# Feed-forward between two attentions: five f32 layers become three f16 products each

## The chip, the cores and the metric

One core of one Trainium2 chip runs the whole program in one launch. The metric is device time in microseconds (us). A core has five engines with a queue each: PE (TensorE: matmuls and transposes through it), DVE (VectorE), ACT (ScalarE), POOL (GpSimd) and SP (SyncE, here only issuing DMAs). They wait for each other through semaphores. A bank of PSUM holds 128 x 512 f32; PE writes there, DVE and ACT read there, POOL does not.

## The reference, cut to what matters

A sequence of 2048 tokens with 128 features goes through four blocks, each followed by a residual and a layer norm:

```python
x = layernorm(x + L0_attn(x))   # 16 heads of 64, causal
x = layernorm(x + L0_ffn(x))    # the part that is changed
x = layernorm(x + L1_attn(x))   # 16 heads of 8, with a Gaussian bias
x = layernorm(x + L1_ffn(x))
# L0_ffn, with tlin(x, w, s) = einsum('bsi,oi->bso', x, w) * s
h = silu(tlin(x, w1, s1)) * tlin(x, w2, s2)          # 128 -> 512, twice
h = gelu(tlin(h, h1, s_h1)); h = gelu(tlin(h, h2, s_h2))   # 512 -> 512, exact gelu
return tlin(h, w3, s3)                                # 512 -> 128
```

The weights are ternary times 8 in the inputs, but the kernel treats them as general f32.

## The kernel before

Three stages stand one after another, each a block of its own whose engines meet at its end.

**First attention.** Eight pairs of heads times four chunks of 512 queries are 32 units; a unit has 4, 8, 12 or 16 turns, one for each 128 keys, so that a pair has 40 turns and the stage 320. In a turn PE makes the scores (three f16 products for each of two heads, `ps_e`), one block of the row maxima of the next unit (`max_products`, bank pair `ps_x`, single: the next block waits until DVE has taken the last, `s_xf`), the product of an earlier turn's probabilities with v, and at most one operation in the bank `ps_y` (`use_y`). ACT makes the exponentials (`exps`, a ring of six buffers), POOL adds them up (`acc`, line L328), DVE reduces the blocks of maxima (`take_max`, L618 and L621) and masks diagonal scores (L697). `plan()` places the operations in `ps_y` by due turns: projections of the next pair (`qk`, `v`), the row sums (`sum`), the output products (`yo`), the turned maxima (`mt`, without which the next unit cannot start), and the transposes of the feed-forward weights (`wt`): eleven groups of four 128 x 128 transposes (w1 and w2 one group each, h1 and h2 four each, w3 one), due at turns 22 and 34 of the pairs 1 to 6. ACT copies a finished `wt` group from `ps_y` to SBUF in f32 and frees the bank; DVE has no part in it.

**Feed-forward.** Four chunks c of 512 tokens. `NH` is 4. For each chunk PE makes, in this order: four outputs of w1 and w2 (`gate_up`, 8 products of 128x128 by 128x512), four outputs of h1 from four inputs (`hidden(c, 0, o)`, 16 products), four of h2 (16), and w3 (`last_layer`, 4): 44 products of f32, 176 in the stage. Between them stand the norm before the next chunk (`n0`), the norm after the last one (`n1`), each with transposes to tokens and back, and the projections q, k, v, f of the second attention for the last chunk, which share one bank `ps_j`. ACT does silu, gelu and the copies of projections; DVE multiplies gate and up (`gated`, L1228), does the norms, `query`, `key`, `value` and the residual; POOL only splits the queries into three bf16 parts (L962 to L968). After the last chunk a chain of small steps prepares the second attention.

**Second attention and last feed-forward.** Not touched.

A line such as `link(ins)` adds one to a semaphore and makes DVE wait for it, so that the next DVE instruction starts only when this one has ended.

## Time and profile before

| | us |
|---|---|
| median of 3 runs | 1796.94 (1796.51 to 1797.92) |
| the profiled execution, its own time | 1798.3 |
| its span, first to last instruction | 1796.6 |
| first attention | 0 to 828 |
| feed-forward, PE's first product to its last | 835.4 to 1005.0 |
| preparation of the second attention | 1005 to 1046 |
| second attention and end | 1046 to 1796.6 |

The profiled execution is one run; 1.7 us of its time lie outside the span. A busy share is to be read by stage, since each stage has its own limit.

### The profile page before, as it was taken

What the parts mean: (1) busy time and instruction counts of PE and PEld (TensorE: products, weight loads), DVE (VectorE), ACT (ScalarE), POOL (GpSimd) and SP (SyncE); (2) the same over time, 40 slices, a digit from 0 to 9 for tenths busy, and PEclk for the clock granted to TensorE, in tenths of its full rate; (3) what the DMA queues carried; (4) which work ended last, traced back from release to release, by engine and by line L of the source; (5) the groups of instructions that cost most, each with busy time, mean ns of one, the idle gap of its engine ahead of it and who ended that gap; (6) DMA issues with size and microseconds to landing.
All of it is one profiled execution on the core that took longest, in us unless ns stands there. A gap on an engine that the chain in (4) does not pass through costs nothing.

```text
span 1796.6 us, 27707 instructions
## 1 busy us (share of the span) xinstructions
PE 1649.1 (92%) x10488; PEld 492.0 (27%) x10488; DVE 1277.0 (71%) x2570; ACT 965.8 (54%) x1109; POOL 670.0 (37%) x408
## 2 busy tenths in 40 slices
PE   7999999999999999995999769999999999999995
PEld 3232323333333323322444311111111111111122
DVE  6767576666667575722233489999999999999974
ACT  2444545444444444442343315777777777777774
POOL 4577877878887878892000110000000000000012
PEclk8999999999999999997999857999999999999998
DMA  4100000000000000001012440111211121111000
GB/s 112 35 9 13 14 13 9 12 13 10 16 7 19 8 16 10 13 13 31 2 36 58 100 94 1 24 24 24 41 24 31 31 46 26 24 23 24 2 2 24
DMA packets 76215, 46.40 MB, mean 26 GB/s; under 512 B 22158, under 2 KB 74930, under 8 KB 76082
## 3 DMA queue, kind: packets, MB, share of 16 engines
q1 hardware_dynamic: 74738, 43.38, 11.4%
q8 instruction: 83, 1.36, 0.3%
q10 hardware_dynamic: 1344, 1.25, 0.2%
q14 instruction: 50, 0.41, 0.1%
HBM read 25.66 MB, written 9.31 MB: 19 GB/s over the span
## 4 chain that ended last, share of the span: by engine, by line
PE 29%; DVE 17%; ACT 3%; DMA 2%; issue 1%; SPq 1%; POOL 0%; DVEq 0%; ACTq 0%; POOLq 0%
DVE maxpart L1717 15%; PE ps_o L1613 9%; PE ps_h L1013 6%; PE ps_r L1575 5%; ACT probs L1534 3%; PE ps_e L1603 2%; DMA qrows<-maxrow 2%; PE ps_g L995 1%; PE ps_u L1000 1%; PE ps_u L1022 1%; PE ps_r L1592 1%; SPq L1456 0%; PE ps_g L1091 0%; PE ps_r L1658 0%; PE ps_j L1044 0%
## 5 line engine op out<-in xcount | busy, mean ns | idle before, releaser
L1717 DVE TENSOR_REDUCE maxpart<-ps_r 128x1 f32<-128x512 f32 x1024 | 634.5, 682 | 26.8 <-PE ps_r L1575 25.9
L1534 ACT ACTIVATE probs<-ps_e 128x1024 f32<-128x1024 f32 x512 | 504.7, 1023 | 194.9 <-PE ps_e L1603 189.8
L328 POOL TENSOR_TENSOR acc<-acc,probs 128x1024 f32<-128x1024 f32 (+3 forms) x256 | 502.9, 1964 | 77.9 <-ACT probs L362 55.3
L362 ACT ACTIVATE probs<-ps_e 128x1024 f32<-128x1024 f32 (+1 forms) x320 | 285.7, 901 | 380.7 <-DVE ps_e L697 131.0
L1575 PE MATMUL ps_r<-krows,qrows 60*128 60x512 bf16 x1024 | 346.9, 402 | 50.8 <-DVE maxpart L1717 17.9
L528 PE MATMUL ps_o<-probs,v 128*64 128x512 f32 (+3 forms) x1280 | 308.6, 561 | 0.2 <-ACT pv_raw L369 0.2
L618 DVE TENSOR_REDUCE maxpart<-ps_x 128x2 f32<-128x1024 f32 x192 | 234.5, 1222 | 75.3 <-PE ps_x L443 75.3
L1603 PE MATMUL ps_e<-qrows,krows 62*128 62x512 bf16 x1024 | 278.8, 386 | 4.2 <-DMA qrows<-maxrow 3.3
L1613 PE MATMUL ps_o<-probs,v 128*9 128x512 f32 x2048 | 269.2, 598 | 12.4 <-ACT probs L1534 12.3
L1499 POOL TENSOR_TENSOR rstd<-veps,power 128x4 f32<-128x4 f32 x8 | 8.1, 1014 | 700.2 <-DVE veps L1767 700.2
L1575 PEld LDWEIGHTS ps_r<-krows,qrows 60*128 60x128 bf16 x1024 | 80.0, 94 | 466.2 <-DVE maxpart L1717 340.4
L621 DVE CUSTOM_DVE_ANT_0 masked<-ps_x,later 128x128 f32<-128x128 f32 (+3 forms) x256 | 115.0, 486 | 60.7 <-PE ps_x L443 59.6
L443 PE MATMUL ps_x<-k_hi,q_hi 64*128 64x512 f16 (+3 forms) x640 | 114.0, 353 | 20.0 <-DVE maxpart L618 16.1
L493 PE MATMUL ps_e<-q_hi,k_hi 64*128 64x512 f16 (+3 forms) x640 | 115.7, 358 | 0.4 <-ACT probs L362 0.3
L493 PE MATMUL ps_e<-q_hi,k_lo 64*128 64x512 f16 (+3 forms) x640 | 112.6, 348 | 0.0
L493 PE MATMUL ps_e<-q_lo,k_hi 64*128 64x512 f16 (+3 forms) x640 | 112.5, 348 | 0.0
L323 POOL TENSOR_TENSOR acc<-probs 128x1024 f32<-128x1024 f32 x32 | 75.3, 2353 | 98.8 <-ACT probs L362 98.8
L528 PEld LDWEIGHTS ps_o<-probs,v 128*64 128x64 f32 x1280 | 63.8, 135 | 86.9 <-issue 77.2
L493 PEld LDWEIGHTS ps_e<-q_hi,k_hi 64*128 64x128 f16 x640 | 30.8, 93 | 158.8 <-issue 103.9
L697 DVE TENSOR_TENSOR ps_e<-ps_e,ahead 128x256 f32<-128x256 f32 (+1 forms) x128 | 55.6, 443 | 23.7 <-PE ps_e L493 15.9
L1603 PEld LDWEIGHTS ps_e<-qrows,krows 62*128 62x128 bf16 x1024 | 59.3, 94 | 32.9 <-ACT probs L1534 10.9
L962 POOL CAST parts_q<-qs 128x512 bf16<-128x512 f32 x4 | 2.4, 609 | 176.1 <-DVE qs L1242 176.1
(258 smaller groups left out, 1368.6 us busy)
## 6 DMA issues: line engine op xcount, KB each, us to landing
qrows<-q_rows SPq DMA_DIRECT2D x64, 192.0 KB
rbc<-rden SPq DMA_DIRECT2D x128, 64.0 KB, 2.1
q_rows<-parts_q SPq DMA_DIRECT2D x24, 128.0 KB, 2.4
k_rows<-parts_k SPq DMA_DIRECT2D x24, 128.0 KB, 2.4
krows<-k_rows SPq DMA_DIRECT2D x16, 192.0 KB, 5.9
w_rows<-parts_w SPq DMA_DIRECT2D x6, 256.0 KB, 2.6
qrows<-a_rows SPq DMA_DIRECT2D x64, 24.0 KB
qrows<-w_rows SPq DMA_DIRECT2D x64, 24.0 KB
```

The lines of the kernel that those rows point to most:

```text
L328: pool.tensor_tensor(acc[:, u % 2, :, o:], acc[:, u % 2, :, o:], probs[:, turn % RING, :, o:], ALU.add)\
L362: act.activation(probs[:, turn % RING, :, o:], ps_e[:, turn % 2, :, o:], ACT.Exp, scale=1.0 / math.sqrt(D0))\
L443: mm = pe.matmul(ps_x[:, h, 0:w], hi["q"][rows, p % 2, (4 * qc + t) * P:(4 * qc + t + 1) * P], hi["k"][rows, p % 2, c * QC:c * QC + w], st ...
L493: mm = pe.matmul(out[:, h, o:], k_part["k"][rows, p % 2, keys], q_part["q"][rows, p % 2, queries], start=n == 0 and turn % 2 == 0, stop=n ...
L528: mm = pe.matmul(ps_o[D0 * h:D0 * h + D0, o:], v[:, p % 2, kt, D0 * h:D0 * h + D0], probs[:, turn % RING, h, o:], start=kt == 0, stop=kt = ...
L618: dve.reduce_max(maxpart[:, u % 2, :, t, c:c + 1], ps_x[:, :, 0:w], AX.X).then_inc(s_xf, 1)
L621: ins = dve.tensor_tensor_reduce(out=masked[:, h, 0:w], in0=ps_x[:, h, 0:w], in1=later[:, QC - w:QC], scale=1.0, scalar=-3e38, op0=ALU.add ...
L1534: act.activation(probs[:, HG * (turn % 2) + hh], ps_e[:, e % 2], ACT.Exp).then_inc(s_ex, 1)
L1575: return pe.matmul(out, qrows[64 * j:64 * j + R_M, u % 3, c, hh, t * P:(t + 1) * P], krows[64 * j:64 * j + R_M, u // NQ % 2, hh, c * KB:(c ...
L1603: mm = pe.matmul(ps_e[:, e % 2, j], krows[64 * j:64 * j + R_END, u // NQ % 2, hh, at * P:(at + 1) * P], qrows[64 * j:64 * j + R_END, u % 3 ...
L1613: mm = pe.matmul(ps_o[32 * hh:32 * hh + D1 + 1, :], v1[:, TU * j + at, HG * (u // NQ) + hh, :], probs[:, HG * (turn % 2) + hh, j, :], star ...
L1717: dve.reduce_max(maxpart[:, at:at + 1], ps_r[:, k, :], AX.X).then_inc(s_bf[k], 1)
```

## The change

All five layers of the feed-forward take three f16 products in place of one f32 product: high weights by high activations, low weights by high activations, high weights by low activations. A high part is the value rounded to f16, the low part what is left, rounded to f16.

Weights: after the transposes ACT writes the high part, and DVE, from the same bank, the low part; only then is `ps_y` free. DVE then also sums the squares of each weight row (`row_norms`), and at turn 296 PE adds these over the partitions (a new operation `bound`) and DVE works out, in a chain of fifteen linked instructions, scale factors that keep the hidden activations inside the range of f16 and folds them into the scales `sc`.

Activations: the input x is copied twice by ACT (f16, then f32) and its low part made by POOL. DVE writes gate times up to `prod` in f32 and then copies it to f16; POOL makes the low part. ACT writes each gelu in f32 and then again, scaled, in f16; POOL scales the f32 one and makes the low part. Rings of two buffers tie these together. PE makes outputs 0 and 1 of a hidden layer together, first all products with high activations, then those with low ones. `last_layer(c-1)` and the residual move behind the first output of the next chunk. The projections q and k now follow each other directly. POOL's splitting of queries comes after the low parts of each chunk.

```diff
@@ first attention: placing, ACT, PE, DVE
+            due.setdefault(TP * (NPAIR - 1) + 16, []).append(("bound", 0))
...
                 elif kind == "wt":
-                    out = wt[name][:, 0, :] if o is None else wt[name][:, :, o * P:(o + 1) * P]
+                    w_hi, w_full = weight_group(i, 0)
                     act.wait_ge(s_yp, n + 1)
-                    act.activation(out, ps_y[:, :] ..., ACT.Copy).then_inc(s_yf, 1)
+                    act.activation(w_hi, w_full, ACT.Copy).then_inc(s_fh, 1)
...
+                elif kind == "bound":
+                    pe.wait_ge(s_nr, 4)
+                    for t in range(4):
+                        for h in range(2):
+                            last = pe.matmul(ps_y[32 * t:32 * t + 32, 0:6 * NH], ones2[:, h, :], norms[...], ...)
...
+            def row_norms(name, o):
+                if name == "w3":
+                    # four tensor_tensor of 128x16 or less, in SBUF
+                    return
+                for t in range(NH) if o is None else (o,):
+                    row = raw[name][:, t, :]
+                    ins = dve.tensor_tensor_reduce(out=squares..., in0=row, in1=row, scale=1.0, scalar=0.0,
+                                                   op0=ALU.mult, op1=ALU.add, accum_out=norms[:, layer, t:t + 1])
+                ins.then_inc(s_sq, 1)
+            def bounds():
+                def inverse_root(out, src, w):
+                    link(dve.tensor_scalar(half[:, 0:w], src.bitcast(I32), 1, None, ALU.arith_shift_right))
+                    link(dve.tensor_scalar(out.bitcast(I32), half[:, 0:w], -1.0, float(ROOT_SEED), ALU.mult, ALU.add))
+                inverse_root(seed[:, 0:2], total[:, 4:6], 2)
+                link(dve.tensor_tensor(total[:, 4:6], total[:, 4:6], seed[:, 0:2], ALU.mult))
+                link(dve.tensor_scalar(most[:, 0:1], total[:, 0:1], float(DM * DM), None, ALU.mult))
+                link(dve.tensor_tensor(most[:, 3:4], most[:, 0:1], total[:, 2:3], ALU.mult))
+                link(dve.tensor_tensor(most[:, 1:2], most[:, 0:1], total[:, 4:5], ALU.mult))
+                link(dve.tensor_tensor(most[:, 2:3], most[:, 3:4], total[:, 5:6], ALU.mult))
+                inverse_root(seed[:, :], most[:, 0:3], 3)
+                link(dve.tensor_scalar(up[:, :], seed[:, :], 2.0 ** 15, None, ALU.mult))
+                link(dve.reciprocal(down[:, :], up[:, :]))
+                for n, col in (("w2", up[:, 0:1]), ("h1", down[:, 0:1]), ("h2", down[:, 1:2]), ("w3", down[:, 2:3])):
+                    link(dve.tensor_scalar(sc[n], sc[n], col, None, ALU.mult))
...
+                elif kind == "wt":
+                    dve.wait_ge(s_fh, i + 1)
+                    dve.tensor_tensor(w_lo, w_full, weight_group(i, 0)[0], ALU.subtract).then_inc(s_yf, 1)
+                    row_norms(*FGROUPS[i])
+                elif kind == "bound":
+                    dve.wait_ge(s_yp, n + 1)
+                    dve.reduce_sum(total[:, :], ps_y[...], AX.X).then_inc(s_yf, 1)
+                    bounds()
@@ feed-forward: POOL
+            def features_low(c):   # waits s_tf, s_xh
+                pool.tensor_tensor(x_part[:, 1, :], xt[:, CHUNK[c]], x_part[:, 0, :], ALU.subtract).then_inc(s_xl, 1)
+            def gated_low(c, o):   # waits s_ah
+                pool.tensor_tensor(a_part[:, 1, o, :], prod[:, n % 2, :], a_part[:, 0, o, :], ALU.subtract).then_inc(s_al, 1)
+            def hidden_low(c, k, o):   # waits s_ha, s_hl, then s_hu, s_hh
+                pool.tensor_scalar(gel_up[:, :], gel[:, n % 2, :], up[:, k + 1:k + 2], None, ALU.mult).then_inc(s_hu, 1)
+                pool.tensor_tensor(part[:, 1, o, :], gel_up[:, :], part[:, 0, o, :], ALU.subtract).then_inc(s_hl, 1)
@@ feed-forward: PE
+            def first_layer(out, name, c, o):
+                pe.matmul(out[:, :], w_hi, x_part[:, 0, :], start=True, stop=False)
+                pe.matmul(out[:, :], w_lo, x_part[:, 0, :], start=False, stop=False)
+                if o == 0:
+                    pe.wait_ge(s_xl, c + 1)
+                return pe.matmul(out[:, :], w_hi, x_part[:, 1, :], start=False, stop=True)
...
+            def hidden(c, k, outs):
+                for o in outs:
+                    if n >= 2:
+                        pe.wait_ge(s_ha, n - 1)
+                    for i in range(NH):       # o == 0: waits s_ah (k = 0) or s_hh (k = 1) for input i
+                        for part in range(2):
+                            pe.matmul(ps_h[n % 2][:, :], w[:, part, i, ...], src[:, 0, i, :], ...)
+                for o in outs:
+                    for i in range(NH):       # o == 0: waits s_al or s_hl
+                        mm = pe.matmul(ps_h[n % 2][:, :], w[:, 0, i, ...], src[:, 1, i, :], ...)
+                    mm.then_inc(s_h, 1)
...
             for c in range(NQ):
-                for o in range(NH):
+                gate_up(c, 0)
+                if c > 0:
+                    last_layer(c - 1)
+                for o in range(1, NH):
                     gate_up(c, o)
...
-                hidden(c, 1, 0)
+                hidden(c, 1, (0, 1))
                 if c > 0:
                     project("q", c - 1)
-                hidden(c, 1, 1)
-                if c > 0:
                     project("k", c - 1)
-                hidden(c, 1, 2)
+                hidden(c, 1, (2,))
@@ feed-forward: ACT and DVE
+                if n >= 2:
+                    act.wait_ge(s_hu, n - 1)
+                act.activation(gel[:, n % 2, :], ps_h[n % 2][:, :], ACT.Gelu, scale=...).then_inc(s_ha, 1)
+                act.wait_ge(s_ha, n + 1)
+                act.activation((b_part, c_part)[k][:, 0, o, :], gel[:, n % 2, :], ACT.Identity, scale=up[...]).then_inc(s_hh, 1)
...
+                if n >= 2:
+                    dve.wait_ge(s_al, n - 1)
+                dve.scalar_tensor_tensor(prod[:, n % 2, :], ps_u[m % 2][:, :], sc["w2"][...], gate[:, n % 2, :], ...).then_inc(s_gu, 1)
+                dve.wait_ge(s_gu, m + 1)
+                dve.tensor_copy(a_part[:, 0, o, :], prod[:, n % 2, :]).then_inc(s_ah, 1)
```

## Rows read from the trace of the kernel before

**Rows 1.** The page: busy time and share of each engine.

```profile
PE 1649.1 (92%) x10488; PEld 492.0 (27%) x10488; DVE 1277.0 (71%) x2570; ACT 965.8 (54%) x1109; POOL 670.0 (37%) x408
```

**Rows 2.** Busy time by stretch, first attention: from:to, length, engines, PE clock.

```profile
230.00:330.00 100.00, 97.98 (x726) 32.51 (x722) 64.75 (x141) 47.78 (x60) 79.85 (x42) 1.00 0.05 12
...
795.00:805.00 10.00, 6.91 (x40) 1.70 (x40) 0.69 (x1) 3.26 (x4) 9.71 (x5) 1.00 0.01 2
```

**Rows 3.** The same view, one chunk of the feed-forward.

```profile
884.40:927.40 43.00, 43.00 (x120) 20.32 (x119) 15.50 (x52) 18.02 (x25) 3.53 (x4) 1.00 0.14 37
```

**Rows 4.** The chain that ended last, in the feed-forward: start, length.

```profile
927.40 10.30 PE ps_h L1013 x24
```

**Rows 5.** Order of time, PE, f16 products in the first attention.

```profile
174.18 0.61 PE L422 MATMUL ps_y<-x_sb,wq_hi 128*128 128x512 f16 x2 [0.56 <-DVE k_lo L652]
174.63 0.38 PE L422 MATMUL ps_y<-x_sb,wq_lo 128*128 128x512 f16 x1
174.94 0.39 PE L493 MATMUL ps_e<-q_hi,k_hi 64*128 64x512 f16 x2
```

**Rows 6.** Groups by line and form, feed-forward: busy, mean ns, idle before.

```profile
L1228 DVE SCALAR_TENSOR_TENSOR act_a<-ps_u,sc_w,gate 128x512 f32<-128x512 f32 x16 | 12.0, 751 | 16.8 <-PE ps_u L1000 16.8
L1122 ACT ACTIVATE x_sb<-ps_h,sc_h 128x512 f32<-128x512 f32 x16 | 11.0, 687 | 35.6 <-PE ps_h L1013 35.6
...
L968 POOL TENSOR_TENSOR parts_q<-qs,parts_q 128x512 bf16<-128x512 f32 x3 | 3.5, 1155 | 0.2
...
L1249 DVE CAST parts_k<-mk 128x512 bf16<-128x512 f32 x3 | 2.5, 830 | 9.8 <-ACT mk L1134 9.8
...
L1213 DVE TENSOR_TENSOR t<-t,veps 128x4 f32<-128x4 f32 x8 | 1.3, 162 | 0.3
L1251 DVE CAST parts_k<-rest 128x512 bf16<-128x512 f32 x3 | 1.3, 426 | 0.1
```

**Rows 7.** The weight transposes by tile: count, duration, first and last start.

```profile
L464 PE MATMUL ps_y<-ident,raw_h x32: 272/273/329, 301.7 to 620.2; 128*128 128x128 f32 x32
...
L464 PE MATMUL ps_y<-ident,raw_w x12: 272/273/329, 204.6 to 690.3; 128*128 128x128 f32 x12
```

**Rows 8.** Order of time at a weight group of turn 22.

```profile
302.38 0.60 ACT L392 ACTIVATE wt_h<-ps_y 128x512 f32<-128x512 f32 x1 [0.69 <-PE ps_y L464]
...
303.36 1.23 DVE L618 TENSOR_REDUCE maxpart<-ps_x 128x2 f32<-128x1024 f32 x1 [0.65 <-PE ps_x L443]
...
305.02 0.22 PE L443 MATMUL ps_x<-k_hi,q_hi 64*128 64x128 f16 x2
...
306.33 2.35 POOL L323 TENSOR_TENSOR acc<-probs 128x1024 f32<-128x1024 f32 x1 [3.83 <-ACT probs L362]
```

**Rows 9.** Order of time at a weight group of turn 34.

```profile
325.30 12.35 POOL L328 TENSOR_TENSOR acc<-acc,probs 128x1024 f32<-128x1024 f32 x5
...
329.38 0.60 ACT L392 ACTIVATE wt_h<-ps_y 128x512 f32<-128x512 f32 x1 [0.57 <-PE ps_y L464]
...
330.35 1.23 DVE L618 TENSOR_REDUCE maxpart<-ps_x 128x2 f32<-128x1024 f32 x1 [2.38 <-PE ps_x L443]
...
331.91 0.38 PE L443 MATMUL ps_x<-k_hi,q_hi 64*128 64x512 f16 x2
```

**Rows 10.** Order of time: a DVE instruction in SBUF beside one of POOL.

```profile
35.96 2.34 POOL L323 TENSOR_TENSOR acc<-probs 128x1024 f32<-128x1024 f32 x1 [10.51 <-ACT probs L362]
35.99 3.40 DVE L687 TENSOR_SCALAR yt<-xt,obias 128x2048 f32<-128x2048 f32 x1
```

**Rows 11.** Groups by form, first attention: DVE with one operand in PSUM.

```profile
L621 DVE CUSTOM_DVE_ANT_0 masked<-ps_x,later 128x512 f32<-128x512 f32 x64 | 41.5, 685 | 22.6 <-PE ps_x L443 22.6
```

**Rows 12.** Order of time around turns 296 to 298.

```profile
759.49 12.36 POOL L328 TENSOR_TENSOR acc<-acc,probs 128x1024 f32<-128x1024 f32 x5
...
762.63 1.23 DVE L618 TENSOR_REDUCE maxpart<-ps_x 128x2 f32<-128x1024 f32 x1
...
766.49 0.38 PE L443 MATMUL ps_x<-k_hi,q_hi 64*128 64x512 f16 x2
```

More of the change, by code:

```diff
@@ L90, in build @@
         masked = sb("masked", [P, 2, QC])
+        squares = sb("squares", [P, NH, P], BF16)
+        norms = sb("norms", [P, 6, NH])
+        total = sb("total", [P, 6])
+        half = sb("half", [P, 3], I32)
+        seed = sb("seed", [P, 3])
+        most = sb("most", [P, 4])
+        down = sb("down", [P, 3])
         ahead = sb("ahead", [P, 2 * P])
@@ L465, in use_y @@
                                             else raw[name][:, o, t * P:(t + 1) * P], ident[:, :])
+                elif kind == "bound":
+                    pe.wait_ge(s_nr, 4)
+                    for t in range(4):
+                        for h in range(2):
+                            last = pe.matmul(ps_y[32 * t:32 * t + 32, 0:6 * NH], ones2[:, h, :],
+                                             norms[:, :, :].rearrange("p r o -> p (r o)"), start=h == 0, stop=h == 1,
+                                             skip_group_check=True)
                 elif kind == "sum":
@@ L876, in build @@
         J_FREE.update({("k", NQ - 1): J_AT["q", NQ - 1] + 1, ("v", NQ - 1): J_AT["q", NQ - 1] + 2})
-        U_W = {(c, o): 5 * c + o for c in range(NQ) for o in range(NH + 1)}
+        U_USES = []
+        for c in range(NQ):
+            U_USES += [(c, 0)] + [(c - 1, NH)] * (c > 0) + [(c, o) for o in range(1, NH)]
+        U_USES += [(NQ - 1, NH)]
+        U_W = {use: m for m, use in enumerate(U_USES)}
         CHUNK = [slice(c * QC, (c + 1) * QC) for c in range(NQ)]
@@ L969, in _ @@
                     .then_inc(s_pq, 1)
+            features_low(0)
+            for c in range(NQ):
+                for o in range(NH):
+                    gated_low(c, o)
+                for o in range(NH):
+                    hidden_low(c, 0, o)
+                for o in range(NH - 1):
+                    hidden_low(c, 1, o)
+                if c + 1 < NQ:
+                    features_low(c + 1)
+                hidden_low(c, 1, NH - 1)
+                if c > 0:
+                    query_parts(c - 1)
+            query_parts(NQ - 1)
         @block.tensor
@@ L987, in to_features @@
                 tr.then_inc(s_tp, 1)
+            def first_layer(out, name, c, o):
+                w_hi, w_lo = [wt_part[name][:, part, 0, o * P:(o + 1) * P] for part in range(2)]
+                pe.matmul(out[:, :], w_hi, x_part[:, 0, :], start=True, stop=False)
[3 more added lines that the diff above has]
+                return pe.matmul(out[:, :], w_hi, x_part[:, 1, :], start=False, stop=True)
             def gate_up(c, o):
@@ L1017, in last_layer @@
             def last_layer(c):
                 m = U_W[c, NH]
+                out = ps_u[m % 2]
                 pe.wait_ge(s_gu, m - 1)
                 for i in range(NH):
-                    pe.wait_ge(s_ha, 2 * NH * c + NH + i + 1)
-                    mm = pe.matmul(ps_u[m % 2][:, :], wt["w3"][:, i, :], act_c[:, i, :], start=i == 0, stop=i == NH - 1)
+                    pe.wait_ge(s_hh, 2 * NH * c + NH + i + 1)
+                    for part in range(2):
+                        pe.matmul(out[:, :], wt_part["w3"][:, part, i, :], c_part[:, 0, i, :], start=i == 0 and part == 0, stop=False)
@@ L1023, in last_layer @@
+                for i in range(NH):
+                    pe.wait_ge(s_hl, 2 * NH * c + NH + i + 1)
+                    mm = pe.matmul(out[:, :], wt_part["w3"][:, 0, i, :], c_part[:, 1, i, :], start=False, stop=i == NH - 1)
                 mm.then_inc(s_u, 1)
@@ L1071, in _ @@
                     project("v", c - 1)
-                hidden(c, 1, 3)
+                hidden(c, 1, (3,))
                 if c > 0:
                     project("f", c - 1)
-                last_layer(c)
+            last_layer(NQ - 1)
             c = NQ - 1
@@ L1279, in _ @@
             for c in range(NQ):
-                for o in range(NH):
+                gated(c, 0)
+                if c > 0:
+                    residual(c - 1)
+                for o in range(1, NH):
                     gated(c, o)
```

145 lines of the change are left out of this document (103 added, 42 removed).

## The prediction, made before the changed kernel was run

> **What bounds the kernel now.** I read the page first: PE is busy for 92% of the span, DVE 71%, POOL 37% [rows 1]. That is a mean over stages, so busy time by stretch comes next. In the middle of the first attention PE is busy 97.98 of 100 us, and POOL already 79.85 [rows 2]. Near its end PE falls to 6.91 of 10 while POOL is at 9.71: there POOL's sums set the pace [rows 2]. In the feed-forward a chunk takes 43.00 us and PE is busy for all 43.00; DVE has 15.50, ACT 18.02 and POOL only 3.53 [rows 3]. So a shorter product shortens this stage at once, until another engine's answer is late. The chain that ended last runs through these products with nothing between them [rows 4].
>
> **Products of the feed-forward.** A hidden output is 4 products, each two records. 24 records take 10.30 us [rows 4], 0.429 each, so one f32 product takes 0.858. An f16 product of the same shape starts 0.225 after the one before (three from 174.18 to 174.63), although one lasts 0.38 [rows 5]. If it took a quarter of the f32 product it would be 0.2146. These are the ends; I take 0.218, between them, because a steady stream should lose less than a group of three. The gain of a product is 0.858 - 3 x 0.218 = 0.204, times 176 = **-36.0 us**, with bounds -32.3 (0.225) and -37.8 (0.2146).
>
> The Trainium skill, "TensorE: Matmul & The Clock Gate", section "Back-to-back issue gap", gives 518 cycles at the full clock, 0.216 us, for 512 columns; the rows lie on both sides of it. By it the gain would be 37 us and the whole sum 1 us lower.
>
> **New waits there.** A result is out 0.16 after PE is free (0.38 - 0.22, [rows 5]) and its reader starts about 0.2 after. ACT needs 0.69 for a gelu and, I take, 0.69 again for the f16 copy; DVE 0.75 for gate times up and 0.43 for a copy, or 0.83 where POOL is running; POOL 1.155 for a difference [rows 6]. POOL's scaling is not in the trace: at least a DVE copy's 0.43, at most its own two-input 1.155; I take 0.6, nearer a one-input instruction. Then:
> - In chunk 0 PE's third product waits for POOL's first low part: two copies of 0.6 (as L392, [rows 8]) in a row and 1.155 put it some 1.2 late.
> - At the start of h1 the last f16 input is ready 0.2 + 0.75 + 0.05 + 0.85 = 1.85 after PE is free. Six products cover 1.3, transposes 0.4 from chunk 1 on. With DVE's 1.5 an output against PE's 1.3, that leaves 0.55 in chunk 0 and 0.6 in each later one.
> - Projection k now follows q in the same bank, with ACT's 0.69 between: 0.2 + 0.69 + 0.04 = 0.93, in three chunks. Before, a hidden output lay there.
> - Output 2 of a hidden layer waits for the gelu of output 0, covered but for 0.1, twice in a chunk.
> - POOL's query splitting delays the next chunk's low parts, 0.4 twice.
>
> At the start of h2 I count nothing: gelu and copy are ready 1.63 after PE is free, and six products with transposes cover 1.7; the low parts are needed after 4.5 and ready after 2.9. `last_layer` is hidden behind the next chunk's first output. Sum: 2.0 + 3 x 1.9 + 0.8 = **+8.5 us**, bounds 3 (only q to k) and 14 (POOL's scaling at 1.155). The preparation at 1005 to 1046 stays: its chain gets no new instruction, and POOL's two splits fit ahead of it.
>
> **Weight groups in the first attention.** Eleven groups, from 204.6 to 690.3 [rows 7], each now have 0.69 of DVE for the low part, then the squares: one instruction of 512 columns (0.68, as L621 of this width, [rows 11]), or four of 128 for w1 and w2. They stand ahead of DVE's next block of maxima, and the next block of PE waits for that one. Two positions repeat.
> - *Turn 22.* ACT's copy ends at 302.98. DVE then works to 303.7 and to 304.45, so the reduction that began at 303.36 begins at 304.5 and ends at 305.7; PE wanted the bank at 305.02 [rows 8]. Stall 0.85. POOL is idle until 306.33. Four h groups: 3.4; w1 1.05 (four short instructions take 0.9); w3 0.9. Together 5.35.
> - *Turn 34.* ACT's copy ends at 329.98, DVE's low part at 330.7, and without any other wait the stall would again be 0.85. But POOL is adding without a break, 2.47 per instruction: one runs from 330.24 to 332.6 [rows 9].
>
> Does the sum of squares wait for it? A DVE instruction that began 0.03 after one of POOL lasted 3.40 [rows 10]: POOL's end at 38.30, and 1.09 more, which is 2048 columns at the rate of L1251's 512 in 0.43 [rows 6]. So it stood until POOL had finished. The same copy takes 0.83 beside POOL and 0.43 alone [rows 6]. Both take two elements at once from SBUF. Instructions with one operand in PSUM are not touched: L621 is 0.685 at 80% POOL [rows 2, 11]. The squares read two streams from SBUF; no row shows such an instruction beside POOL. Bounds: no wait, or a wait for the end of POOL's instruction. I take the wait, since two SBUF elements per step is what the two delayed forms share. Then DVE gets to the squares at 332.6, the reduction ends at 334.4 instead of 331.57, and PE, which wanted the bank at 331.91 [rows 9], stalls 2.55. Four h groups: 10.2. In w2 the first of four short instructions waits likewise, POOL then takes one more addition of 2.35, after which it has no input, since PE has stopped: 5.2. Together 15.4, against 4.45 without the wait.
>
> The Trainium skill, "SBUF — State Buffer", section "SBUF: two separate sides", says that DVE and GpSimd share one pair of ports as an exclusive lock, held for a whole instruction, and that a DVE instruction with two SBUF inputs needs it too. The trace agrees for the two delayed forms (3.40 and 0.83) and has no row for two inputs. With the rule this part is 20.8 us, without it 9.8.
>
> **The chain of scales.** At turn 296 DVE is free at 763.86 [rows 12]; its reduction of PE's sums ends about 764.4. Fifteen linked instructions at 0.2 (0.16 and 0.04 idle, L1213, [rows 6]) are 3.0. Four are two-input ones in SBUF, and POOL is adding from 759.49 to 771.85 [rows 12]. Two of them wait, to 766.8 and 769.3; then POOL is out of input, because PE, wanting the bank at 766.49 [rows 12], waits for the reduction behind the chain. It ends at 771.5, the reduction at 772.75. PE loses 6.1, POOL, which sets the pace from here, **5.3**. Without the wait: 1.3.
>
> **Sum.** -36.0 + 8.5 + 20.8 + 5.3 = -1.4. The profiled execution took 1798.3, so 1796.9; it lies 1.4 above the median 1796.94. Carried to the median: **1795.5 us**.
>
> **Rivals.**
> - *DVE's two-input instructions don't wait for POOL* (0.20). For it: no row shows the wait in this form. Against it: rows 10 and the copies. Attention costs 9.8 + 1.3 = 11.1: -36.0 + 8.5 + 11.1 = -16.4, 1780.5 us.
> - *POOL becomes the bound of the feed-forward* (0.12), slower. Scaling at 1.155 makes 8 x 2.4 + 5 x 1.2 + 3.5 = 28.7 us of POOL in a chunk, and if some ten DVE instructions of 0.43 to 0.69 hold it up, 34 to 35, against PE's 43.00 - 44 x 0.204 = 34.0. From 34 on POOL decides, and late low parts stop PE at each layer; 3 us more a chunk, 12 in all: +10.6, 1807.5 us. Against it: the copies alone delay POOL by under 3 us.
> - *The clock falls* (0.05). It is 1.00 through the stage [rows 3]; waits of 1 to 2 us at each layer could lower it. If a quarter of its 142 us, 35, pass at half the clock, half of that is lost, 18: 1813.5 us. The 6 us wait at turn 298 is the likeliest place.
>
> **How the numbers follow.** The forecast has 0.63. Its own range is 1786 to 1803: products -1.8 to +3.7, waits +-5, attention +-5, put together +-8. The rivals carry it to **1778 to 1806**, which leaves out under 0.07 below and 0.13 above. A measurement tells from no change about 0.2%, 3.6 us. Of the forecast 0.23 lie more than that below, 0.28 within, 0.12 above; the first rival adds 0.19 below and 0.01 within, the second 0.01 within and 0.11 above, the third 0.05 above: faster 0.42, same 0.30, slower 0.28.
>
> **What would show it.** Feed-forward from PE's first product to its last: 142 us (169.6 before, less 36.0, plus 8.5), records of about 0.22, PE busy some 95%. k's product 0.9 after q's copy. The squares of h groups at turn 34 about 2.4 us long, at turn 22 0.6; PE idle before L443's counterpart 2.5 and 0.85. The scale chain 7 us long with two instructions of over 2 us. First attention 26 us longer; from the feed-forward's end to the end of the program no difference. I am wrong if the squares take 0.6 everywhere (then 1780), if PE doesn't wait on `ps_x` after them, or if low parts from POOL end PE's waits in the hidden layers.

## The result, and the profile after

The changed kernel takes 1810.68 us (median of 4, 1809.69 to 1811.82); the kernel before took 1797.26 in the same comparison. The ratio is 1.0075, 95% interval 1.0058 to 1.0092: slower by 13.4 us, and outside the predicted range of 1778 to 1806 with its 1795.5. The profiled execution took 1810.6, its span 1808.9. By stage, from the starts of the same instructions in both traces:

| stage | before | after | difference | predicted |
|---|---|---|---|---|
| first attention and norm, to the first product of the feed-forward | 835.4 | 866.0 | +30.6 | +26.1 |
| feed-forward, first to last product | 169.6 | 155.9 | -13.7 | -27.5 |
| preparation, to the first product of the slides | 16.6 | 15.9 | -0.7 | 0 |
| second attention and end | 775.0 | 771.1 | -3.9 | 0 |

The page of the changed kernel. Against [rows 1] POOL has gone from 37% to 43%. In `PEclk`, the granted clock of PE by slice, there are digits of 8 in slices 18 to 20, where the kernel before has 9, 7 and 9. A new group stands among the costliest, POOL's scaling.

```profile
PE 1626.2 (90%) x10680; PEld 476.3 (26%) x10680; DVE 1324.5 (73%) x2649; ACT 989.8 (55%) x1145; POOL 782.4 (43%) x492
...
PEclk8999999999999999988899856999999999999998
...
L1073 POOL TENSOR_SCALAR gel_up<-gel,up 128x512 f32<-128x512 f32 x32 | 51.3, 1603 | 21.2 <-ACT gel L1288 18.0
```

**First attention, turn 34.** Timeline of the changed kernel where it stands at an h group (start, us), to be read against [rows 9]:

```profile
333.08 7.60 POOL L351 TENSOR_TENSOR acc<-acc,probs 128x1024 f32<-128x1024 f32 x3
...
335.30 0.69 DVE L731 TENSOR_TENSOR wt_h_parts<-ps_y,wt_h_parts 128x512 f16<-128x512 f32 x1 [2.04 <-ACT wt_h_parts L414]
...
335.91 2.58 DVE L681 CUSTOM_DVE_ANT_0 squares<-raw_h 128x512 bf16<-128x512 f32 x1
...
338.42 1.22 DVE L646 TENSOR_REDUCE maxpart<-ps_x 128x2 f32<-128x1024 f32 x1
339.69 0.39 PE L464 MATMUL ps_x<-k_hi,q_hi 64*128 64x512 f16 x2 [2.32 <-DVE maxpart L646]
...
340.33 1.57 PE L556 MATMUL ps_o<-probs,v 128*64 128x512 f32 x4
```

The squares take 2.58 us where POOL is adding without a break, and 0.68 at turn 22 [rows 8], where it is idle; the reduction behind them is late and PE stands for 2.32. That is the forecast (2.4, 0.6, stall 2.5) within 0.2 us. The last line was not forecast: the four products with v take 1.57 us, not 1.08. Granted clock by stretch (the third number from the end; 1.00 is 2.4 GHz):

```profile
336.00:342.00 6.00, 3.68 (x22) 0.74 (x20) 5.20 (x5) 0.69 (x2) 4.54 (x2) 0.90 0.00 0
342.00:348.00 6.00, 6.00 (x42) 1.77 (x40) 3.71 (x9) 2.48 (x4) 4.44 (x3) 0.82 0.00 0
795.00:805.00 10.00, 9.76 (x45) 2.25 (x47) 4.19 (x12) 3.07 (x3) 6.27 (x4) 0.67 0.00 0
...
238.00:244.00 6.00, 5.94 (x36) 1.69 (x38) 2.92 (x9) 1.83 (x2) 2.62 (x2) 0.72 0.00 0
...
544.00:550.00 6.00, 6.00 (x50) 1.79 (x46) 4.98 (x11) 2.60 (x4) 3.71 (x2) 1.00 0.00 0
```

Behind four of the five stalls of turn 34 the mean clock of 6 us is 0.72: 3.4 us at the half level, 1.2 GHz, which cost 1.7 us each; the third h group (544 to 550) kept 2.4 GHz, after the same stall of 2.32. Behind the stall of the scale chain it is 0.67 over 10 us, which cost 3.3. So 10 us of the 30.6 are clock. The rest: PE's waits for DVE on `ps_x` between 200 us and the end of the stage rose from 6.3 to 29.2 us, by 22.9, and its waits for POOL at the end fell from 15.6 to 13.6. 22.9 + 10.1 - 2.0 = 31.0, against 30.6.

This sum takes only the places named. Over the whole stage, from its start and in steps of 1 us (PE's busy time, times what the granted clock lacks to 1.00), the clock cost 20.2 us, against 12.4 before: 7.7 more, because the opening, before 80 us, lost only 6.5 where it had lost 9.8. PE's waits on `ps_x` from the start rose by 24.3. 24.3 + 7.7 - 2.0 = 30.0. What the opening loses differs from trace to trace (8.0 in that of e1 below) without an edit there, so 2 to 3 us of such a difference can be chance.

**The scale chain.** Two instructions waited for POOL, the rest took 0.15 to 0.25; PE's stall is 6.38 us (6.1 forecast from [rows 12]):

```profile
786.45 2.37 DVE L696 TENSOR_SCALAR half<-total 128x2 int32<-128x2 int32 x1
...
789.05 2.23 DVE L700 TENSOR_TENSOR total<-total,seed 128x2 f32<-128x2 f32 x1
...
795.24 0.61 PE L464 MATMUL ps_x<-k_hi,q_hi 64*128 64x512 f16 x2 [6.38 <-DVE maxpart L646]
```

The first has one input, two int32 per partition.

**Feed-forward.** The stage as a whole, PE's waits in it (us in total, times, longest), and the timeline around the start of the second chunk:

```profile
866.00:1021.90 155.90, 138.68 (x618) 62.23 (x618) 67.20 (x181) 89.53 (x123) 118.96 (x93) 0.97 0.14 33
```

```profile
PE ps_h L1167 <- POOL x_sb L1076: 6.4, 4, 1.9
PE ps_g L1130 <- POOL x_part L1060: 4.8, 2, 4.0
PE ps_h L1157 <- DVE a_part L1401: 2.8, 5, 0.9
PE ps_j L1203 <- ACT mq L1298: 2.3, 3, 0.8
```

```profile
900.30 1.56 POOL L1073 TENSOR_SCALAR gel_up<-gel,up 128x512 f32<-128x512 f32 x1 [0.17 <-POOL c_part L1076]
...
901.95 1.15 POOL L1076 TENSOR_TENSOR c_part<-gel_up,c_part 128x512 f16<-128x512 f32 x1
903.06 1.15 POOL L1060 TENSOR_TENSOR x_part<-xt,x_part 128x512 f16<-128x512 f32 x1
...
904.27 0.61 PE L1130 MATMUL ps_g<-x_part,wt_w_parts 128*128 128x512 f16 x1 [4.02 <-POOL x_part L1060]
```

Before, PE was busy for all 169.6 us and POOL for 10.58 (the chunk in [rows 3] is typical); now PE is busy for 138.68 of 155.9 and POOL for 118.96. The products became as short as forecast (0.2156 apart, sixteen in 3.45 us, against half of the 0.429 between records in [rows 4]), but PE stands for 17.2 us, two thirds of it (11.6) for POOL. One hidden output costs POOL 1.56 + 1.155 and two waits, 2.97 us, against PE's 2.6. The scaling, taken as 0.6 and bounded by 1.155, took 1.56. The low parts of h2's inputs are late by 1.5 to 1.9 in each chunk. The low part of x for the second chunk is late by 4.02, and behind that the clock is at the half level until 907.3.

### The profile page after: what moved, and what is told of

The parts are those of the page before. It is cut to its first block, busy times and chain, and to the rows that moved or that the text cites. A ratio compares the mean times of both kernels' runs of the same rounds, so it can differ in the third digit from the quotient of the medians.

```text
span 1808.9 us, 28389 instructions
## 1 busy us (share of the span) xinstructions
PE 1626.2 (90%) x10680; PEld 476.3 (26%) x10680; DVE 1324.5 (73%) x2649; ACT 989.8 (55%) x1145; POOL 782.4 (43%) x492
## 4 chain that ended last, share of the span: by engine, by line
PE 22%; DVE 19%; POOL 4%; ACT 4%; issue 2%; DMA 0%; SPq 0%; DVEq 0%; POOLq 0%; ACTq 0%
DVE maxpart L1892 17%; PE ps_o L1788 9%; PE ps_r L1750 6%; ACT probs L1709 3%; POOL gel_up L1073 2%; PE ps_e L1778 2%; POOL x_sb L1076 1%; PE ps_h L1157 1%; PE ps_h L1167 1%; PE ps_r L1767 1%; POOL c_part L1076 1%; PE ps_g L1251 0%; PE ps_j L1203 0%; ACT gel L1288 0%; PE ps_r L1833 0%
## 5 line engine op out<-in xcount | busy, mean ns | idle before, releaser
L556 PE MATMUL ps_o<-probs,v 128*64 128x512 f32 (+3 forms) x1280 | 313.1, 569 | 0.2 <-ACT pv_raw L392 0.2
L1788 PE MATMUL ps_o<-probs,v 128*9 128x512 f32 x2048 | 268.4, 596 | 12.4 <-ACT probs L1709 12.2
L1073 POOL TENSOR_SCALAR gel_up<-gel,up 128x512 f32<-128x512 f32 x32 | 51.3, 1603 | 21.2 <-ACT gel L1288 18.0
```

The source lines that it names most:

```text
L556: mm = pe.matmul(ps_o[D0 * h:D0 * h + D0, o:], v[:, p % 2, kt, D0 * h:D0 * h + D0], probs[:, turn % RING, h, o:], start=kt == 0, stop=kt = ...
L1788: mm = pe.matmul(ps_o[32 * hh:32 * hh + D1 + 1, :], v1[:, TU * j + at, HG * (u // NQ) + hh, :], probs[:, HG * (turn % 2) + hh, j, :], star ...
```

## The experiments

Sixteen kernels ran; where nothing else is said, each is the changed kernel with one edit. Times are medians; ratios are to the kernel before, which took 1796.4 to 1797.6 beside them.

| run | us | ratio (95%) | edit |
|---|---|---|---|
| e1 | 1793.28 | 0.9977 (0.9967 to 0.9986) | one-input instruction for the squares |
| e2 | 1789.05 | 0.9953 (0.9938 to 0.9968) | squares by ACT |
| e3 | 1806.35 | 1.0053 (1.0038 to 1.0068) | scale chain in the feed-forward |
| e4 | 1797.85 | 1.0004 (0.9994 to 1.0013) | low parts of gelus by DVE |
| e5 | 1810.33 | 1.0075 (1.0059 to 1.0092) | POOL scales by a constant |
| e6 | 1800.49 | 1.0022 (1.0012 to 1.0031) | POOL scales by a two-input product |
| e7 | 1814.81 | 1.0101 (1.0086 to 1.0116) | k later, low part of x earlier |
| e12 | 1814.33 | 1.0096 (1.0082 to 1.0110) | k later |
| e8 | 1771.92 | 0.9862 (0.9847 to 0.9876) | e2, e3, e4 and k later |
| e9 | 1769.10 | 0.9844 (0.9831 to 0.9858) | e2, e3, e4 |
| e10 | 1767.98 | 0.9837 (0.9823 to 0.9850) | e9 with q earlier |
| e11 | 1766.11 | 0.9828 (0.9815 to 0.9842) | e10 with the chain split |
| e13 | 1813.35 | 1.0084 (1.0067 to 1.0101) | 32 bytes of SBUF unused |
| e14 | 1796.61 | 0.9992 (0.9982 to 1.0001) | kernel before, 32 bytes unused |
| e15 | 1763.43 | 0.9811 (0.9796 to 0.9825) | e11 with 32 bytes unused |
| e16 | 1763.44 | 0.9808 (0.9794 to 0.9823) | e11 with 96 bytes unused |

### Does DVE wait for POOL, and what does the clock add?

```diff
-                    ins = dve.tensor_tensor_reduce(out=squares..., in0=row, in1=row, ..., accum_out=norms[:, layer, t:t + 1])
+                    ins = dve.reduce_max(aside[:, layer, t:t + 1], row, AX.X)   # norms: constants
```

> In place of the sums of squares of weight rows stands, on the same engine at the same place, a maximum over the same 512 (or 128) elements: one SBUF input instead of two, about the same 0.68 us alone. The norms are then constants (the sum of squares is left out), everything else stays. Theory (DVE's two-input instruction waits until POOL's running instruction ends, and PE's stall at turn 34 of 2.32 us, 4.69 for w2, is followed by some 6 us of lower clock that cost 1.6 more): the instruction takes 0.6 to 0.7 us at turn 34 too, PE's stall there falls to about 0.3, the clock in the 6 us behind it is 1.00, and the kernel gains 4 x (2.0 + 1.6) + 5.5 = about 20 us: 1790. Rival (DVE simply has too much to do at that place): the stall stays near 2.3 and the time near 1810. Second rival (the lock is right but the clock would have fallen anyway): about 12 us gained, 1798.

Measured: 17.4 us less, between the 20 of the theory and the 12 of the second rival. The instruction, the sum of PE's waits on `ps_x`, and the stretches that had 0.90 and 0.82:

```profile
L683 DVE TENSOR_REDUCE aside<-raw_h x8: 674/676/677, 303.9 to 625.7; 128x1 f32<-128x512 f32 x8
...
PE ps_x L466 <- DVE maxpart L648: 17.0, 21, 6.4
...
336.00:342.00 6.00, 6.00 (x52) 1.89 (x50) 4.91 (x13) 1.88 (x4) 5.34 (x3) 1.00 0.00 0
342.00:348.00 6.00, 4.77 (x39) 1.57 (x37) 4.64 (x8) 3.38 (x5) 3.18 (x3) 1.00 0.01 3
```

Same place, same engine, same 512 elements, same load on POOL: all eight take 0.68, the stall behind one of them is 0.41, and the clock stays at 2.4 GHz. DVE's load is not the cause. Two things differ between the instructions: the squares have a second SBUF input, and they write 512 values to SBUF where the maximum writes one. Writing is not it: the low part at 335.30 above writes 512 values to SBUF while POOL is adding, and takes 0.69. Nor is it the form: the masked maxima of [rows 11] are of the same form as the squares, with one operand in PSUM, and take 0.685 beside POOL. That leaves the second input. Of the 16.9 us by which the feed-forward starts earlier (849.1), 12.2 are waits. 4.7 are left for the clock, whose stretches above come to 6.8; of the difference of 2, 1.5 is lost in the opening, where the clock cost 8.0 in this trace and 6.5 in that of the changed kernel. The Trainium skill, "SBUF — State Buffer", section "Who interferes with whom", says that a DVE instruction with two SBUF inputs contends with a GpSimd instruction that reads SBUF, and that one with at most one SBUF input does not, unless it runs in a mode that uses two ports. The traces agree (2.58 against 0.68; 0.69 for the low part, which has one input in SBUF and one in PSUM).

```diff
+                    act.activation(squares..., raw[name][:, t, :], ACT.Square, accum_out=norms[:, layer, t:t + 1])
-                    ins = dve.tensor_tensor_reduce(...)
```

> The squares are summed by ACT (Square with accumulation) right behind its f16 copy of the group, not by DVE. Nothing is left out. Theory of the lock: DVE has only its low part with one operand in PSUM, so turn 34 stalls no more, and the 0.9 at turn 22 shrinks too. ACT reads 512 elements in about 0.7 us, which puts the next exponential 0.7 later; ACT is busy 55%, so most of it is hidden. Expected gain 17 to 21 us: 1790 to 1794. Rival: the exponential behind it is late for PE's next turn by 0.5 in eleven places: 1796.

Measured: 21.6 us less. ACT takes 0.62 and 0.19 for a group, and PE's waits on `ps_x` are 13.1, of which 6.4 belong to the scale chain:

```profile
L421 ACT ACTIVATE squares<-raw_h x8: 621/622/622, 302.1 to 620.2; 128x512 bf16<-128x512 f32 x8
L421 ACT ACTIVATION_READ_ACCUMULATOR squares<-raw_h x8: 192/193/194, 302.6 to 620.8; 128x1 f32 x8
...
PE ps_x L473 <- DVE maxpart L655: 13.1, 11, 6.4
```

### The scale chain

```diff
@@ DVE, first attention, at "bound"
-                    bounds()
@@ DVE, feed-forward
             norm("n0", 0)
+            bounds()
```

> The chain of fifteen linked scale instructions is moved from turn 296 of the first attention to the beginning of the feed-forward, behind the first norm on DVE, where POOL is idle and PE and ACT are busy with the features and the first layer for some 3 us. The sums (four matmuls and one reduction) stay. Theory: PE's stall of 6.38 us at turn 298 falls to under 1, and the half clock behind it (0.67 over 795 to 805) goes, which gives back 6 + 2 to 3 = 8 to 9 us; the chain, some 3.0 us without a wait, holds up the first product of gate and up by at most 1 us. 1802 to 1804. Rival: POOL sets the pace there anyway, so that only part of PE's stall was ever paid: 1806 or more.

Measured: 4.3 us less in the whole, but the feed-forward starts 8.6 earlier (857.4). With POOL idle, the two instructions of over 2 us take 0.16, and the clock behind the old place is 1.00:

```profile
855.49 0.16 DVE L1411 TENSOR_SCALAR half<-total 128x2 int32<-128x2 int32 x1
...
855.89 0.16 DVE L1415 TENSOR_TENSOR total<-total,seed 128x2 f32<-128x2 f32 x1
...
795.00:805.00 10.00, 9.81 (x74) 2.88 (x68) 2.28 (x6) 5.34 (x8) 9.43 (x7) 1.00 0.01 2
```

So of 6.4 of stall and 3.3 of clock most was paid. The rival (POOL sets the pace there anyway) accounts for 1.8: PE's waits for POOL at the end of the stage rose from 13.6 to 15.4. Of the 8.6, 1.8 went in the feed-forward, where the first products of gate and up now wait 1.0 for the chain, and 2.5 to a longer second attention, which led to the last four runs.

### Who holds up the feed-forward?

```diff
-                pool.tensor_scalar(gel_up, gel, up[:, k + 1:k + 2], None, ALU.mult)
-                pool.tensor_tensor(part[:, 1, o, :], gel_up, part[:, 0, o, :], ALU.subtract)
+                dve.scalar_tensor_tensor(part[:, 1, o, :], gel, up[:, k + 1:k + 2], part[:, 0, o, :], ALU.mult, ALU.subtract)
```

> POOL's two instructions for each low part of a hidden activation (scaling 1.56, difference 1.155, with waits 2.97 in all) become one of DVE: gelu times scale less the f16 part, 0.75 us as the one that multiplies gate and up. 32 of them. POOL keeps the low parts of x and of gate times up and the queries. Nothing is left out. Theory (POOL's scaling was mis-sized, POOL is late for the low parts and paces h1): POOL's busy time in the feed-forward falls from 119 to about 30 us, PE's waits of 1.5 to 1.9 for h2's low part of input 3 and the one of 4.02 for the low part of x go, with the half clock behind it; the feed-forward takes 143 to 148 us instead of 155.9: about 1800. Rival (DVE, busy with norms and queries, is late in its turn): PE waits for DVE's low parts as long as for POOL's, and the time stays at 1808 to 1812.

Measured: 12.8 us less. From first to last product 141.1 us, where the prediction had 142, PE busy for 135.05 of them, POOL for 35.41; no wait for POOL in h1 or h2 is left:

```profile
868.90:1010.00 141.10, 135.05 (x618) 62.41 (x618) 85.43 (x214) 89.47 (x123) 35.41 (x32) 0.98 0.19 44
...
PE ps_j L1187 <- ACT mq L1282: 2.4, 3, 0.8
PE ps_g L1114 <- POOL x_part L1060: 1.0, 2, 0.7
```

Which property of POOL's scaling costs 1.56 us?

```diff
-  pool.tensor_scalar(gel_up, gel, up[:, k + 1:k + 2], None, ALU.mult)
+  pool.tensor_scalar(gel_up, gel, (2.0 ** -17, 2.0 ** -26)[k], None, ALU.mult)            # e5
+  pool.tensor_tensor(gel_up, gel, up[:, k + 1:k + 2].to_broadcast([P, QC]), ALU.mult)    # e6
```

> POOL multiplies the gelu by a constant in the instruction (2 to the -17, 2 to the -26) instead of the computed scale that it reads from a column; the low parts are then not those of the scaled activations. Nothing else changes. What makes POOL's scaling 1.56 us? Theory A (the scale read from a column): the instruction falls to 1.1 us or less, POOL's 32 instructions lose 15 us or more, and since POOL paces h1 and is late for h2, the feed-forward gets 6 to 10 us shorter: 1801 to 1805. Theory B (POOL's tensor_scalar in f32 has this rate anyway, 3.05 ns for each column against 2.25 for its two-input difference): 1.56 again and 1810.7 again.

> POOL's scaling is written as a product of two tensors, the second the column of the scale repeated over 512 elements. The result is the same. Theory: it takes what POOL's difference takes, 1.155 us instead of 1.56, so 0.4 less for each hidden output; POOL's pair is then 2.5 us with its waits, under PE's 2.6 for an output, and PE's waits for h2's low part and for the low part of x shrink by 1 to 2 us each: 6 to 9 us gained, 1802 to 1805. Rival (what holds PE up is the latency of ACT's two instructions and POOL's two in a row, not their rate): 2 to 3 us gained.

The instruction in the one and in the other (ns, least, median, most):

```profile
L1073 POOL TENSOR_SCALAR gel_up<-gel x32: 1486/1488/1886, 882.7 to 1018.4; 128x512 f32<-128x512 f32 x32
```

```profile
L1073 POOL TENSOR_TENSOR gel_up<-gel,up x32: 1038/1039/1445, 882.6 to 1008.6; 128x512 f32<-128x512 f32 x32
```

Reading the scale from a column costs 0.07 of the 1.56, and without it the time does not move (1810.3). The form costs the rest: the product of two tensors does the same work in 1.04. POOL's pair, with its waits, then takes 2.42 instead of 2.97, less than PE's 2.6 for an output; no wait of PE for h2's low parts is left, the stage takes 143.4 us, and 10.2 us are gained in the whole, more than the 6 to 9 expected. The latency rival, which had 2 to 3, is out. The count of inputs doesn't set the price either: POOL's cast of the same 128x512 from f32 to bf16, one input, takes 0.61 (L962 of the kernel before).

### Order

```diff
@@ PE (e7, e12)
                     project("q", c - 1)
-                    project("k", c - 1)
                 hidden(c, 1, (2,))
+                    project("k", c - 1)
@@ POOL (e7): features_low(c + 1) ahead of hidden_low(c, 1, 2), not behind it
```

> Only the order of work in the feed-forward changes: PE makes projection k behind output 2 of h2, not directly behind q in the same bank, and POOL makes the next chunk's low part of x one hidden output earlier. Theory: PE's three waits of 0.78 for ACT's copy of q go (2.3 us), the wait of 4.02 for the low part of x at 904 falls by POOL's 2.97 for a hidden output, with about half of the half clock behind it: 5 to 7 us gained, 1804 to 1806. Rival (POOL paces the stage, so time won at one wait is lost at the next wait for POOL): 1 to 3 us, 1808 to 1810.

> The changed kernel with projection k behind output 2 of h2 and nothing else: the half of the earlier run on order (1814.8) that has nothing to do with POOL's order. Theory (there the low part of x, moved forward in POOL's queue, made POOL stand idle 1.7 us in each chunk until ACT had copied x, while POOL paces the stage): k alone costs at most 1 us: 1809 to 1812. Rival (the position of k is what cost 4 us): 1814 to 1815.

Both failed: 4.1 and 3.7 us more. In e12 the three waits of 0.78 for q are gone, and others came: f waits 1.44 for DVE to empty v, which now stands close ahead of it, and v 0.34 for ACT's copy of k.

```profile
942.29 1.13 PE L1201 MATMUL ps_j<-mq,l_wfq 128*128 128x512 f32 x2 [1.44 <-DVE v L1431]
```

In e7 POOL, which paces the stage, stands idle for 1.68 in the second and in the third chunk until ACT has copied x. PE's wait of 4.02 does shrink, to 1.1, but from the first projection q to the second 41.6 us pass instead of 38.4, and from the second to the third 39.9:

```profile
939.25 1.53 POOL L1060 TENSOR_TENSOR x_part<-xt,x_part 128x512 f16<-128x512 f32 x1 [1.68 <-ACT xt L1271]
```

The feed-forward is 5.0 us longer in the profile of e7 (160.5 from the first product's start to the last one's, against 155.5) and 0.8 in that of e12. The medians put e12 as high as e7. The profiled run of e12 took 1811.9 at a mean clock of 0.957, its other three runs 1814.3 to 1815.9 at 0.951 to 0.953. So part of what e12 costs shows as clock; why it fell in those runs is open.

### The edits together

> Four edits at once, nothing left out: ACT sums the squares, the chain of scales stands at the start of the feed-forward, DVE makes the low parts of hidden activations in one instruction each, and projection k stands behind output 2 of h2. Singly the first three gave 21.6, 4.3 and 12.8 us. If they add up, with 2 for k: 1810.7 - 40.7 = 1770. If the one takes the other's gain away (DVE's chain of scales now delays its low parts in the first chunk; the second attention is some 3 us longer in some kernels than in others): 1775.

> The four edits together without the one of projection k: ACT sums the squares, the chain of scales stands at the start of the feed-forward, DVE makes the low parts of hidden activations; q and k follow each other as in the changed kernel. In the run with all four, PE waited 3.6 us for DVE to empty v and 1.5 for ACT's copy of k, in place of 2.4 for ACT's copy of q. Theory (k behind output 2 pushes v and f together, so that f waits for DVE): 2 to 4 us less than 1771.9: 1768 to 1770. Rival (the position of k costs nothing): 1772.

> The three edits, and projection q one step earlier, ahead of the first two outputs of h2, with ACT's copy of it ahead of the first gelu of h2; k stays where it is. Theory: PE's three waits of 0.78 for ACT's copy of q go and v and f keep their places: 2.3 us less than with three edits. Rival (ACT's copy now delays the f16 activations that PE needs at the start of h2): no gain.

> As the run before, and in the first chunk DVE does only the scale of w2 ahead of its first product of gate and up; the other four instructions of the chain follow that product, and DVE's preparations for the second attention (constants, 4.2 us) follow the fourth. In the run with four edits PE waited 1.17 for the first product, then 0.52 and 0.91, and the clock was half until 841. Theory: PE's wait of 1.2 goes: 1 to 3 us less. Rival (h1's start takes it over, or the norm of the second chunk, which the preparations now delay): no gain.

The gains of e2, e3 and e4 add up: 1810.7 - 21.6 - 4.3 - 12.8 = 1772.0 was to be expected, and e9 gives 1769.1, 27.7 less than the kernel before beside it. Its feed-forward starts at 834.9, where that of the kernel before starts (835.4): what the change had cost the first attention is gone. e8, with k later, is 2.8 us above e9. e10 (2.3 expected) and e11 give 1.1 and 1.9 more, hardly beyond what runs differ by, but in the profiles the stage shrinks in step (142.7, 140.3, 138.7 between the first and the last product's start).

### The second attention, which nobody touched

From PE's first slide product to the end: 771.1 us in the changed kernel and 770.4 to 771.1 in e1, e2, e4 to e7 and e12; 773.4 to 773.6 in e3 and e8 to e11; 775.0 in the kernel before. The groups differ in where the buffers `krows` and `qrows` lie: at a multiple of 256 bytes in the first, 32 bytes off a multiple of 64 in the others, by their allocated addresses. In e13 and e14 an unused buffer shifts them:

```diff
     up = mid.enter_context(nc.sbuf_tensor("up", [P, 3], F32))
+    mid.enter_context(nc.sbuf_tensor("apart", [P, 8], F32))
```

> The changed kernel with one unused buffer of 32 bytes in each partition behind the scale up; nothing else. It moves everything allocated later by 32 bytes: krows and qrows, into which the second attention's transfers write, go from a multiple of 256 bytes back to 32 bytes behind a multiple of 64, where they lie in the kernel before. So far the second attention (from PE's first slide product to the end) took 770.4 to 771.1 us in eight kernels with the multiple of 256 and 773.4 to 775.0 in the kernel before and the five with an offset of 32. Theory (the place of these two buffers sets how long the transfers take, and they end waits at each unit): 2.5 to 4 us slower than the changed kernel, 1813 to 1815, landing of krows 5.3 to 5.9 us instead of 4.3. Rival (something else that these kernels share): 1810.7.

> The kernel before with one unused buffer of 32 bytes in each partition behind the scales: krows and qrows come to lie on a multiple of 64 bytes (64 behind one of 256). Theory: the second attention takes about 771 instead of 775.0 us, and the kernel 1793. Then 4 us of the difference between the two kernels have nothing to do with the products. If only a multiple of 256 helps: 1797. Rival (no effect of the place): 1797.

> The best kernel so far (ACT sums the squares, chain of scales in the feed-forward and split, DVE makes the low parts, q early), whose krows and qrows lie 32 behind a multiple of 64, with 32 bytes more: a multiple of 64. Theory: 1766.1 less 2.8 = 1763. Rival: 1766.

> The same with 96 bytes more: krows and qrows on a multiple of 512. If the multiple of 64 is all that counts: as the run with 32 more, 1763. If a multiple of 256 or 512 gives more: 1 to 3 us less than that.

| kernel | offset from a multiple of 256 | landing of krows, us | second attention, us |
|---|---|---|---|
| changed, e16 | 0 | 4.4, 4.5 | 771.1, 770.3 |
| e15 | 192 | 5.7 | 770.9 |
| e14 (kernel before, shifted) | 64 | 5.4 | 773.8 |
| e11 | 160 | 5.5 | 773.4 |
| e13 | 32 | 6.0 | 773.3 |
| before | 32 | 5.9 | 775.0 |

The row of these transfers in the pages of the changed kernel, of e13 and of e16 (number, size, median us to landing):

```profile
krows<-k_rows SPq DMA_DIRECT2D x16, 192.0 KB, 4.4
```

```profile
krows<-k_rows SPq DMA_DIRECT2D x16, 192.0 KB, 6.0
```

```profile
krows<-k_rows SPq DMA_DIRECT2D x16, 192.0 KB, 4.5
```

The changed kernel with 32 unused bytes more takes 2.7 us more (its runs 1811.9 to 1813.8, against 1809.7 to 1811.8), and 2.2 more in the stage. The pages show where: the products `ps_e` of the second attention, in the kernel before, the changed one and e13 (the last numbers are PE's idle time before them and what ended most of it):

```profile
L1603 PE MATMUL ps_e<-qrows,krows 62*128 62x512 bf16 x1024 | 278.8, 386 | 4.2 <-DMA qrows<-maxrow 3.3
```

```profile
L1778 PE MATMUL ps_e<-qrows,krows 62*128 62x512 bf16 x1024 | 279.0, 385 | 1.2 <-ACT probs L1709 0.9
```

```profile
L1779 PE MATMUL ps_e<-qrows,krows 62*128 62x512 bf16 x1024 | 277.9, 385 | 3.9 <-DMA qrows<-maxrow 3.0
```

In the kernel before and in e13 PE waits 14 times for the transfer that writes the row maxima into `qrows`, in the changed kernel once, for 0.3. That fits the shift as far as these three go. The rest fits less well. e11 has 0.9 us of such waits and e15 0.4, yet the stage is 2.5 shorter in e15. The medians of those two differ by 2.7, but their runs overlap (1764.6 to 1767.6 and 1762.7 to 1765.7). e16, with 96 bytes, is no faster than e15 with 32. In the kernel before the shift to a multiple of 64 gave 1.0 us in the median (ratio 0.9992, 0.9982 to 1.0001) and 1.2 in the stage, where 4 had been expected. So of the 3.9 us between the two kernels the shift accounts for 2.2 by e13 and 1.2 by e14, and the rest is open. Open is also what exactly the shift changes, since it moves every buffer allocated later and not only these two.

Nor is the landing of `krows` the measure: over all eighteen kernels it is 4.3 to 4.9 us at a multiple of 256 and 4.9 to 6.0 elsewhere, and e2 and e9, both with 4.9, have 770.8 and 773.4 in the stage. The Trainium skill, "DMA: Bandwidth & Descriptors", section "How a descriptor splits into AXI transactions", says of reads that a transaction must start at a multiple of 256 bytes, and that a descriptor which starts elsewhere also fetches bytes that it doesn't use. What moves here is where transfers write, for which no run shows that rule.

## Why the prediction was wrong, point by point

**The step that failed** is in "New waits there": POOL's scaling "at least a DVE copy's 0.43, at most its own two-input 1.155; I take 0.6, nearer a one-input instruction". It took 1.56 (e5: 1.49 even with a constant). The upper bound rested on the thought that one input can't cost more than two; e6, at 1.04 for the product of two tensors, shows that here it does. From it followed "low parts are needed after 4.5 and ready after 2.9", so that the start of h2 was counted as nothing; it waits 1.5 to 1.9 in each chunk. Four low parts in a row also cost POOL 2.97 each against PE's 2.6, so that it fell further behind with each. PE waited 17.2 us in the stage, 11.6 of them for POOL, where the prediction had 8.5 in all, 2.0 of them for POOL. In e6, with 1.04, the stage took 143.4, near the 142 of the forecast.

The stage is 23.5 us longer than its products alone would make it (169.6 - 37.2 = 132.4). Besides the 17.2 of waiting, the clock cost 4.8 us in it against 2.8 before, and at each of the 16 waits 0.16 passes in which the last product runs out and PE still counts as busy, some 2.6; 1.7 is not traced. The items of the prediction's own sum add up to 8.0, not 8.5 (a later chunk's are 0.6 + 0.93 + 0.2 = 1.73, not 1.9), which changes nothing in the outcome.

The second rival, POOL as the bound of the feed-forward, had the right mechanism and too low a chance (0.12). It too had the scaling at 1.155, and took the rest from DVE standing in POOL's way, of which the median of 1.155 for POOL's differences shows nothing. Its 1807.5 and the 1813.5 of the third rival, the clock, enclose the result, which holds something of both. e4 takes this work from POOL, and the stage takes 141.1. That this is nearly the forecast's 142 confirms the products, not its list of waits: PE stands for 6.1 us in e4, not 8.5, and in part for other things.

**Products:** right. 0.2156 apart, against 0.218 taken; -37.2 instead of -36.0.

**k behind q:** 0.78 in three chunks against 0.93. **Start of h1:** 2.8 in all, against 2.35.

**Weight groups:** the mechanism was right and its size nearly so (stall 2.32 against 2.55 for h, 4.69 against 5.2 for w2; at turn 22 0.32 against 0.85). In all these groups cost 16.5 us of waiting, not 20.8. The first rival (no wait for POOL) is refuted by e1. What was missing is a term, put at nothing: behind four of these five stalls PE's clock fell, 1.7 us each, 6.8 together. The stage came out only 4.5 above its forecast because 4.3 too much of waiting hid nearly half of the 10.1 of clock, which is luck.

**Scale chain:** 6.38 us of stall against 6.1, two waits of over 2 us as forecast. Their number was right partly by luck: the prediction let only the two-input instructions wait, and the first that waited has one input. The clock behind it cost 3.3 more. The third rival had named this place, but as a case by itself with a chance of 0.05, where it belonged into every case with a stall.

**Second attention:** "no difference" was wrong by -3.9 us, of which the shift of buffers explains 2.2 by e13 and 1.2 by e14; the rest is open.

## What to carry to other kernels

When a change hands work to an engine that the trace shows idle, that engine's price for the new form is the first thing to bound, and a bound taken from an instruction with more inputs is none: here `tensor_scalar` on POOL cost half as much again as `tensor_tensor`. A stall of PE of over 2 us should be priced with the time at half clock behind it, here 1.7 to 3.3 us behind five of the six that the change brought to the first attention. Sums that can be made by ACT, or by DVE with one input, don't collide with POOL; moving them (e2), the low parts (e4) and the chain (e3) turned a change that lost 13 us into a kernel 28 us faster than the one before (e9); the order of q, the split chain and the 32 bytes brought it to 34 (e15).

## What was unexpected of the hardware

- POOL, 128x512 f32: `tensor_scalar` 1.56 us with the scalar in a column and 1.49 with a constant, `tensor_tensor` with a repeated column 1.04, difference of two tensors 1.155, cast to bf16 0.61.
- DVE's wait for POOL also hits a `tensor_scalar` on two int32 in each partition (2.37 us beside POOL, 0.16 without), so smallness is no protection.
- Of the five stalls of 2.3 to 4.7 us at turn 34, four were followed by a stretch at 1.2 GHz, which cost 1.7 us each; one of 0.41 (e1) was not. Behind one of 6.38 it cost 3.3 us, behind one of 4.02 in the feed-forward 1.6.
- The second attention took 2.2 us more (e13) or 2.5 less (e15) when 32 unused bytes moved the buffers behind them in SBUF; in the kernel before it took 1.2 less (e14).
